# Issuing each step of a node update one edge group ahead of its waiter, with two tiles in flight

## The reference, cut to what matters

```python
for l in range(2):                                   # N=3125 nodes, E=100000 edges, D=128, H=8, FF=512
    q, k, v = (linear maps of layernorm(x) and of the node degree)
    att = einsum(q[dst], k[src]) / scale             # per edge and head, clipped to +-50
    ex = exp(att - m[dst]);  alpha = ex / segment_sum(ex, dst)[dst]
    aggr = segment_sum(v[src] * alpha, dst)          # edges and one self loop per node
    x = x + (aggr @ Wo + bo)
    h = gelu(layernorm(x) @ W1 + b1)
    x = x + (h @ W2 + b2)
out = layernorm(x0 + x)
```

## The kernel before

| group | DVE | PE | ACT |
|---|---|---|---|
| even | prod ... att, add_ffn(k-1), one-hots, evacuate, msg, normalise_x3(k-1), share_out(k) | gather_q, sum_further, sum_pair, transpose_z2(k-1), transpose_ag(k), project_next(k-1), project_out(k) | weights, scale_x3(k-1), copy_z2T(k-1), copy_agT(k), one_hots |
| odd | next_row(k-1), add_attention(k), prod ... att, normalise_x2(k), one-hots, evacuate, msg | gather_q, sum_further, transpose_z1(k), hidden(k), sum_pair, project_ffn(k) | scale_x2(k), weights, copy_z1T(k), gelu(k), one_hots |

## Time and profile before

### The profile page before, as it was taken

The page is one execution under the profiler, slowest core; times in us unless marked ns, Lnnn a source line. Parts: engine busy times, 40 slices in busy tenths (PEclk is TensorE's granted clock), DMA queues, the critical chain, the costliest instruction groups (busy, mean ns, idle before and its releaser), DMA issues.

```text
span 2410.0 us, 44174 instructions
## 1 busy us (share of the span) xinstructions
PE 1539.5 (64%) x11737; PEld 1367.1 (57%) x11738; DVE 1474.6 (61%) x2506; ACT 921.0 (38%) x1652; POOL 1506.8 (63%) x1584
## 2 busy tenths in 40 slices
PE   6656555666677676667664556555666666666766
PEld 4545554555666665566653455555555566655665
DVE  8685556566565565656647656565665666555665
ACT  3232222223444454445533222322334444444543
POOL 2557777777776565556407777777777666565550
PEclk8776778677788788889876767777788888787787
DMA  3444555555444444434305555555544444343430
GB/s 76 129 144 158 158 157 158 156 157 159 151 148 134 124 137 125 121 118 135 95 9 173 158 155 157 162 158 157 157 152 152 136 133 129 115 131 117 123 118 5
DMA packets 120426, 321.52 MB, mean 133 GB/s; under 512 B 31458, under 2 KB 43862, under 8 KB 120348
## 3 DMA queue, kind: packets, MB, share of 16 engines
q0 software_dynamic: 75072, 205.10, 28.7%
q1 hardware_dynamic: 44438, 113.89, 14.7%
q10 hardware_dynamic: 838, 1.60, 0.3%
HBM read 311.92 MB, written 8.55 MB: 133 GB/s over the span
## 4 chain that ended last, share of the span: by engine, by line
POOL 29%; PE 26%; issue 16%; DVE 14%; ACT 7%; DVEq 5%; ACTq 2%; DMA 1%; POOLq 0%; SPq 0%
POOL kv L529 29%; PE ps L1280 12%; PE ps L1266 7%; DVE msg L1067 3%; DVE prod L1041 3%; ACT dist L657 2%; DVEq L345 2%; ACT hotT L660 2%; DVE dots L1044 2%; PE ps L1237 2%; DVE q_parts L800 1%; PE ps L1254 1%; PE ps L1243 1%; ACT L629 1%; DVE spot L974 1%
## 5 line engine op out<-in xcount | busy, mean ns | idle before, releaser
L529 POOL DMA_INDIRECT kv<-kv_tab,src_idx x1564 | 1482.4, 948 | 792.8 <-issue 457.0
L1280 PE MATMUL ps<-msg,hot 128*128 128x136 f32 x3904 | 670.8, 339 | 333.6 <-DVE msg L1067 292.5
L1266 PE MATMUL ps<-q_parts,hotT 128*128 x5856 | 562.9, 271 | 451.8 <-DVE prod L1041 256.8
L1280 PEld LDWEIGHTS ps<-msg,hot 128*128 128x128 f32 x3904 | 619.8, 241 | 376.6 <-DVE msg L1067 188.4
L1266 PEld LDWEIGHTS ps<-q_parts,hotT 128*128 x5856 | 499.4, 124 | 512.6 <-issue 492.1
L1041 DVE TENSOR_TENSOR prod<-kv,ps 128x1024 f32<-128x1024 f32 x196 | 239.2, 1220 | 294.3 <-DMA kv<-kv_tab,src_idx 263.7
L949 DVE SCALAR_TENSOR_TENSOR hot<-dst_col,neg_base,ps 128x1024 f32<-128x1024 f32 x244 | 312.0, 1279 | 127.5 <-issue 124.6
L657 ACT ACTIVATE dist<-dst_rows,neg_node 128x1024 bf16<-128x1024 int32 x244 | 280.1, 1148 | 152.3 <-issue 137.7
L664 ACT ACTIVATE msg<-att 128x64 f32<-128x64 f32 x196 | 49.1, 250 | 619.5 <-DVE att L1051 617.4
L660 ACT ACTIVATE hotT<-dist 128x1024 bf16 x244 | 257.8, 1057 | 44.6 <-ACT dist L657 43.7
L1067 DVE TENSOR_TENSOR msg<-kv,ps 128x1024 f32<-128x1024 f32 x196 | 238.1, 1215 | 22.8 <-issue 19.3
(11 more groups left out here) (205 smaller groups left out, 1154.3 us busy)
## 6 DMA issues: line engine op xcount, KB each, us to landing
dst_rows<-in_dst SPq DMA_DIRECT2D x194, 512.0 KB, 4.1
kv<-kv_tab,src_idx POOLq DMA_INDIRECT x1564
kv_tab<-qkv SPq DMA_DIRECT2D x27, 128.0 KB
kv_tab<-qkv SPq DMA_DIRECT2D x3, 768.0 KB, 3.7
out<-z SPq DMA_DIRECT2D x25, 64.0 KB
dst_rows<-in_dst SPq DMA_DIRECT2D x2, 336.0 KB, 3.6
hot<-in_L_gnn_W SPq DMA_DIRECT2D x2, 256.0 KB
w<-in_L_gnn_W SPq DMA_DIRECT2D x2, 256.0 KB
```

Of the source, the lines that this page charges most:

```text
L529: pool.indirect_dma_start(kv[:, u, c, :], None, kv_tab[l][:, :], bass.IndirectOffsetOnAxis(ap=src_idx[:, c, at(g)], axis=0)).then_inc(kv_i ...
L1266: last = MM(qd[:, c * P:(c + 1) * P], hotT[:, bass.ds(pr % 2, 1), c * P:(c + 1) * P], q_parts[:, at(t), k * D:(k + 1) * D], start=first an ...
L1280: last = MM(agg, hot[:, u % 2, c, :], msg[:, u % 2, c, :], start=(c == 0), stop=(c == GC - 1))
```

## The change

The steps of a slot keep their work and move to other places in the groups: each is issued about a group before the step on another engine that waits for it, so that a slot now spans five groups and two tiles are under way at once. With k the slot of the even group and its odd follower:

| group | DVE | PE | ACT |
|---|---|---|---|
| even | prod ... att, share_out(k), one-hots, msg, evacuate, next_row(k-2) | gather_q, sum_further, hidden(k-1), transpose_ag(k), project_next(k-2), sum_pair, project_ffn(k-1), project_out(k) | copy_z1T(k-1), copy_z2T(k-2), weights, copy_agT(k), gelu(k-1), one_hots |
| odd | prod ... att, add_ffn(k-1), add_attention(k), one-hots, msg, evacuate, normalise_x3(k-1), normalise_x2(k) | gather_q, sum_further, sum_pair, transpose_z2(k-1), transpose_z1(k) | weights, scale_x3(k-1), scale_x2(k), one_hots |

`evacuate` also moves from before `msg` to behind it, in all groups. DVE's loop over the slot groups has twelve groups instead of four. Buffers x3, z1T and z2T are added, PSUM banks are dealt anew, SP stores a slot's row one group later, and the slot table takes tiles that are finished one group earlier than before. The core of the diff:

```diff
-        in_slot = {"agT": bank(5, P), "o": bank(5, P), "z1T": bank(4, P), "h": [ps[:, 5, c * P:(c + 1) * P] for c in range(FC)],
-                   "y": bank(6, P), "z2T": bank(4, P), "qkv": bank(6, 3 * D)}
+        in_slot = {"agT": bank(5, P), "o": bank(5, P), "z1T": bank(5, P), "h": [ps[:, 6, c * P:(c + 1) * P] for c in range(FC)],
+                   "y": bank(6, P), "z2T": bank(4, P), "qkv": bank(4, 3 * D)}
...
-                link(nc.vector.tensor_copy(least, low[:, a:b:2]))
-                link(nc.vector.tensor_tensor(least, least, low[:, a + 1:b:2], ALU.min))
+                link(nc.vector.tensor_copy(least, low[:, a - 1:b - 1:2]))
+                link(nc.vector.tensor_tensor(least, least, low[:, a:b:2], ALU.min))
...
+                # ACT
+                def edge_group(word, d, g, u, r, n, slot=None):
+                    even, odd = (slot is not None and u % 2 == k for k in (0, 1))
+                    if even and not_before(slot, 1):
+                        copy_z1T(slot - 1, 0, in_slot)
+                    if even and not_before(slot, 2):
+                        copy_z2T(slot - 2, 0, in_slot)
+                    weights(u, g)
+                    if odd and not_before(slot, 1):
+                        scale_x3(slot - 1, 0)
+                    if odd and opens(slot):
+                        scale_x2(slot, 0)
+                    if even and opens(slot):
+                        copy_agT(slot, 0, in_slot)
+                    if even and not_before(slot, 1):
+                        gelu(slot - 1, 0, in_slot)
+                        log_and_exp()
+                    if not isinstance(g, int) or g + 2 < NG:
+                        one_hots(word, d + 2, r, n)
...
                     # DVE
                     nc.vector.tensor_tensor(att[:, :], clipped[:, :], not_nan[:, :], ALU.mult).then_inc(att_done[l], 1)
-                    if odd and not closing:
-                        normalise_x2(slot, 0)
-                    if even and not opening:
+                    if even and opens(slot):
+                        share_out(slot_tile(dve, slot), slot, 0)
+                        wait_for_number(dve, ag_done[l], slot + 1)
+                    if odd and not_before(slot, 1):
+                        passed = slot_tile(dve, slot - 1)
                         add_ffn(passed, slot - 1, 0, in_slot)
+                    if odd and opens(slot):
+                        add_attention(slot_tile(dve, slot), slot, 0, in_slot)
...
                     one_hot(u, g, tile_of(dve, a, shift))
-                    if not opened:
-                        evacuate(a, last_shift)
                     if ahead:
                         word(d + 1)
                     dve.wait_ge(exp_done[l], g + 1)
                     nc.vector.tensor_tensor(half[:, :, 0:D]...).then_inc(msg_done[l], 1)
-                    if even:
-                        if not opening:
-                            normalise_x3(passed, slot - 1, 0)
-                        if not closing:
-                            dve.wait_ge(evac_done[l], a + 2)
-                            share_out(current, slot, 0)
+                    if not opened:
+                        evacuate(a, last_shift)
+                    if odd and not_before(slot, 1):
+                        normalise_x3(passed, slot - 1, 0)
+                    if odd and opens(slot):
+                        normalise_x2(slot, 0)
+                    if even and not_before(slot, 2):
+                        next_row(slot_tile(dve, slot - 2), slot - 2, 0, in_slot)
...
+                with dve.Fori(2 * FIRST_SLOT // TURN_OF_DVE + 1, 2 * SLOT_END // TURN_OF_DVE) as i:
+                    word = pair_words(dve, TURN_OF_DVE * i)
+                    for u in range(TURN_OF_DVE):
+                        edge_group(u % SLOTS, ..., ahead=u < TURN_OF_DVE - 1, slot=number + u // 2)
...
                     # PE, after gather_q and sum_further
+                    if even and not_before(slot, 1):
+                        hidden(slot - 1, 0, in_slot)
+                    if even and opens(slot):
+                        transpose_ag(slot, 0, in_slot)
+                    if even and not_before(slot, 2):
+                        project_next(slot - 2, 0, in_slot)
                     pe.wait_ge(msg_done[l], g + 1)
                     sum_pair(u, word(d - 1)[0])
+                    if even and not_before(slot, 1):
+                        project_ffn(slot - 1, 0, in_slot)
+                    if even and opens(slot):
+                        project_out(slot, 0, in_slot)
+                    if odd and not_before(slot, 1):
+                        transpose_z2(slot - 1, 0, in_slot)
+                    if odd and opens(slot):
+                        transpose_z1(slot, 0, in_slot)
```

More of the change, by code:

```diff
@@ L163, in gnn_program @@
         rsum = sb("rsum", [P, TAIL, H])
-        one_of_each = {name: sb(name, [P, D]) for name in ("ag", "agT", "x2", "z2", "zT")}
+        one_of_each = {name: sb(name, [P, D]) for name in ("ag", "agT", "x2", "x3", "z1T", "z2", "z2T")}
         spot = sb("spot", [P, TAIL, 2, 10])
@@ L358, in after, with not_before, opens @@
                 eng.wait_ge(semaphore, n)
+        def not_before(slot, n):
+            return not isinstance(slot, int) or slot >= n
+        def opens(slot):
+            return not isinstance(slot, int) or slot < NSLOT
         def slot_tile(eng, j):
@@ L461, in _ @@
                         store(slot_tile(sp, n), 0)
-                for n in range(NSLOT - 2, NSLOT):
+                for n in range(NSLOT - 3, NSLOT):
                     ready(n + 1)
@@ L614, in copy_z1T @@
                     act.wait_ge(z1T_ps[l], n + 1)
-                    nc.scalar.activation(zT[s], banks["z1T"], ACT.Copy).then_inc(z1T_done[l], 1)
+                    nc.scalar.activation(z1T[s], banks["z1T"], ACT.Copy).then_inc(z1T_done[l], 1)
                 def gelu(n, s, banks):
@@ L836, in slot_words_out @@
                 link(nc.vector.tensor_scalar(last, last, float(NT - TAIL), None, ALU.min))
-                for g in (NG - 2, NG - 1):
+                for g in range(2 * SLOT_END - 1, NG):
                     link(nc.vector.tensor_tensor(last, last, low[:, g:g + 1], ALU.min))
@@ L1019, in next_row, with edge_group @@
                                                        in1=banks["qkv"].unsqueeze(1), op0=ALU.mult, op1=ALU.add).then_inc(next_done, 1)
-                def edge_group(u, i, g, word, d, ahead=True, slot=None, opening=False, closing=False):
+                def edge_group(u, i, g, word, d, ahead=True, slot=None):
                     half = msg[:, u % 2, :, :]
                     b, shift = word(d)
-                    odd = slot is not None and u % 2 == 1
-                    even = slot is not None and u % 2 == 0
-                    if even:
-                        if not opening:
-                            passed = slot_tile(dve, slot - 1)
-                        if not closing:
-                            current = slot_tile(dve, slot)
-                    if odd:
-                        if not closing:
-                            current = slot_tile(dve, slot)
-                        if not opening:
-                            next_row(slot_tile(dve, slot - 1), slot - 1, 0, in_slot)
-                        if not closing:
-                            add_attention(current, slot, 0, in_slot)
+                    even, odd = (slot is not None and u % 2 == k for k in (0, 1))
                     last_group = isinstance(g, int) and g == NG - 1
@@ L1236, in hidden @@
                     for c in range(FC):
-                        last = MM(banks["h"][c], w1g[:, l, c * P:(c + 1) * P], zT[s], start=True, stop=True)
+                        last = MM(banks["h"][c], w1g[:, l, c * P:(c + 1) * P], z1T[s], start=True, stop=True)
                     last.then_inc(h_ps[l], 1)
@@ L1286, in sum_further, with pe_group @@
                             sum_pair(u, pr)
-                def pe_group(u, g, word, d, more=True, slot=None, opening=False, closing=False):
-                    odd = slot is not None and u % 2 == 1 and not closing
-                    even = slot is not None and u % 2 == 0
+                def pe_group(u, g, word, d, more=True, slot=None):
+                    even, odd = (slot is not None and u % 2 == k for k in (0, 1))
                     if more:
@@ L1329, in _ @@
                 word = pair_words(pe, 0)
-                pe_group(0, NG - 2, word, NG - 2, slot=NSLOT, closing=True)
-                pe_group(1, NG - 1, word, NG - 1, more=False)
+                for g in range(NG - 2, NG):
+                    pe_group(g % SLOTS, g, word, g, more=g < NG - 1, slot=NSLOT)
+                project_next(NSLOT - 1, 0, in_slot)
                 sum_further(1, word(NG - 2)[0], word(NG - 1)[0])
```

94 lines of the change are left out of this document (29 added, 65 removed).

## The result

The changed kernel takes 2220.97 us (median of four runs, 2219.82 to 2223.71) where the kernel before takes 2409.41 us (four runs; the 2408.93 us above is of three of them); the ratio is 0.922, with a 95% interval from 0.9204 to 0.9236. The forecast was 2222 us. The profiled execution has a span of 2217.9 us at a mean clock of 0.804 (0.778 before).

The account below looks back on a forecast made before the run. PE, ACT, PE round trips and late sums that make DVE wait bound the slot stages, above POOL's 480 us a layer. (612 - 518) + (602 - 512) + 3 = 187 saved from 2412.0 gives 2225, 2222 at the median; range 2160 to 2300.

Parts of the forecast that it names:

- The slot of three kinds: Two-group slots priced by extra pair: none 20.0 us, in the even group 21.0, in the odd 22.1; 505.7 us together.
- other idle time, kept as it was: DVE's idle time in a slot besides the priced waits, such as sequencer work: 3.0, 3.6 or 3.4 us by kind.
- added reads: Slot tile numbers now read by DVE in mid-group, behind a wait: 1.0 us more a slot.
- waits for PE: DVE's remaining waits: 0.6 or 1.7 us in slots with an extra pair, plus 12 us a layer for PE's clock.
- rival 4: The next_row wait only moves to add_attention; only the evacuation gains, 53 us a layer: 2303 us, chance 0.04.
- three steps are missing: Layer 1's slot stage lacks three steps and has one more add: 512 us against layer 0's 518.
- The loop of twelve: DVE's loop over twelve groups: fewer table re-reads at turn heads book 7 us gained; cold straight code costs 5 a layer.
- rival 5: Larger loop body stalls 1.23 us at each branch, 89 us in all: 2311 us, chance 0.04.
- The closing groups: After the slot groups, group 96's 5 us wait goes and next_row comes behind group 97: -3 us a layer.
- POOL's floor everywhere: Both slot stages fall to POOL's 480 us: time 2155 us, chance 0.12.
- PE the bound: PE stays at its lower clock half the time, a slot costs 24 us: about 2347 us, chance 0.11.
- a closed ring: ACT's z copies block its exponentials, making msg late in each slot: 2462 us at 5 us a slot, chance 0.05.

Follow-up runs that it names:

- e1: The changed kernel with add_attention(k) put back to the head of the odd group, ahead of prod: 2380.38 us, ratio 0.9868 to the kernel before.
- e2: The changed kernel with the evacuation put back ahead of msg: 2260.1 us, ratio 0.9365 to the kernel before.
- e3: The kernel before with only the evacuation moved behind msg: 2350.27 us, ratio 0.9745.
- e4: The changed kernel with DVE's loop over four groups instead of twelve: 2224.26 us, ratio 0.9219 to the kernel before.
- e5: The changed kernel with DVE's table reads moved behind the issue of prod and of the reduction, on a slow chip: 3372.68 us, ratio 0.9898.
- e12: The changed kernel with early table reads and next_row(k-2) moved to the odd group, a repeat on a slow chip: 3329.3 us, ratio 1.0003.
- e9: The changed kernel with early table reads and next_row(k-2) moved to the odd group, run again on another slow chip: 3331.77 us, ratio 1.0015.

## Why the prediction was right

**Where the time is, and the floor.** The slot stages alone gave, as the prediction read from the windows; the plain stage did not move.

**The slot of three kinds.** By the starts of prod, the 24 slots of layer 0 take on average 19.3 us without an extra pair (six, priced at 20.0), 21.2 with one in the even group (eleven, 21.0) and 23.1 with one in the odd group (seven, 22.1). Together that is 511 us; the prediction had 505.7 + 12 = 518. The first kind goes below POOL's 20.0 (18.1 in the window of groups 78 and 79), since POOL had run ahead while slots with extra pairs were slow; the price of 20.0 as a floor for each slot was too strict.

**The terms.** Added up over the 24 slots, the prediction's terms and what the profile of the changed kernel shows for them are (us, layer 0):

| term | booked | measured |
|---|---|---|
| DVE busy | 370.8 | 367.7 |
| other idle time, kept as it was | 81.4 | 50.9 |
| added reads | 24.0 | 47.8 |
| waits for PE | 30.5 | 44.6 |
| POOL's floor in the slots without an extra pair | 10.2 | 0 |
| sum | 517 | 511.0 |

The mechanism was right; four of the five sizes were off by 10 to 31 us, two up and two down. With the two that were too small put right alone, the stage would have been forecast at some 555 us, with the two that were too large at 476. That the sum is within 7 us is in part luck.

**The evacuation and next_row.** 52.9 to 15.5 us and 92.2 to 19.3 us. "The next_row wait gone" was too much: it stands in 13 of the slots, 0.9 to 2.5 us long, where PE is behind. e1 and e2 put single steps back, for 155 and 35 us. The evacuation alone, which rival 4 priced at 53 us a layer, gives 62 us in both (e3).

**The added reads** were booked at 1.0 us a slot and measure about 2: 14.9 + 14.6 + 7.2 us of issue before rsum, x2 and x3, and 11.1 us before the one-hot behind wait_for_number, 47.8 us for 24 slots. The idle time that was "kept" made up for it: the issue before the one-hot fell from 28.1 to 20.0 (heads of turns, booked elsewhere), that before prod from 13.2 to 4.0 us, DVE's 8.7 us wait for ACT's scale is not among the waits any more, and 6.9 us of issue before msg are gone; against them 10.2 us of waits for gathers stand where 3.8 did.

**PE.** Booked at 12 us a layer over the waits of the slot kinds (0.6 x 11 + 1.7 x 7 = 18.5), 30.5 in all; DVE's waits for PE add up to 19.3 + 15.5 + 5.4 + 3.3 + 1.1 = 44.6 us in layer 0. The clock rose from 0.82 to 0.87 in that stage and PE's busy time fell from 425.7 to 391.9 us, so PE is busy 77% of the stage, not over 80% as expected. With e1's wait put back it is 0.80 in that stage again, and 0.84 with most of next_row's left (e3); e2 and e4 have 0.88 and 0.89. So the long waits had cost PE its clock, and that they went made PE cheaper. (The sum of 3.34 us from which the factor 1.6 was taken ran at a mean of 0.61, so it is a little under the price of the lower level.)

**Layer 1** was expected 6 us under layer 0 and is 6 us over it. The step that failed there is "three steps are missing": it counted their work as gained. With next_row gone, DVE is at the prod of the odd group 0.8 us after the end of msg instead of 2.1 (means of 23 slots), and so comes to add_ffn earlier; PE's FFN projection stands behind the sum, which waits for msg, and ends 5.3 us after msg instead of 5.0, though PE has less to do. So DVE waits there for PE, 33.1 us against 5.4 in layer 0. A step that is left out on the engine that waits gives little when the result it waits for comes no sooner.

**The loop of twelve** was booked at -7 for its heads and +10 for cold code. Neither is what was measured. The heads are 14 us a layer on DVE, of which e4 shows nothing in the median; the cold code is some 4 to 5 us in the run. The price of 1.23 us was read from a row that shows something else: what stands at 997.38 in the earlier trace rows is no stall at a branch but ACT's second table load of the slot (L629), and the instruction behind it starts as it ends:

```profile
997.32 1.28 ACT L629 ACT_TABLE_LOAD   x1
998.61 1.15 ACT L657 ACTIVATE dist<-dst_rows,neg_node 128x1024 bf16<-128x1024 int32 x1
```

So none of the rows of the kernel before shows a stall of this kind, though the prediction says that the trace agrees with one; the term of 5 us a layer and rival 5's 89 us were built on it. The Trainium skill, "Runtime: NRT & Kernel Launch", section "Instruction fetch mechanics", has straight code fetched ahead and a taken branch outside the held blocks stall. The trace of the changed kernel agrees, with 77 packets against 41 and 1.0 to 1.36 us at the back edges. Rival 5 would have needed 1.23 us at each of the branches in between. There, the heads of turns aside, no gap of issue in layer 0 is over 1.04 us.

**The closing groups** were booked at -3 us a layer: layer 0 gave 5.4 us behind its slot groups, layer 1 nothing (48.8 us to the end instead of 48.0).

**Rivals.** 1 (POOL's floor everywhere, 2155): the stages stay 31 and 37 us above it, and behind group 53 DVE waits for no gather, so POOL is not what holds them. Whether DVE's reads or PE's order gives next was to be told by e5 to e12 and is not settled; e4 says that both do. 2 (PE the bound): not at twice the price for half the time; DVE's waits for PE are 44.6 of 511 us, and the clock rose. 3 (a closed ring): ACT's exponentials are not late; msg waits for ACT once, 0.2 us. 4: refuted by DVE's 1.1 us of waiting for the attention output, and by e2, which gains 153 us without the evacuation's move. 5: see above.

## What to carry to other kernels

Where an engine that works in order asks another for a result, look at what stands in its queue between the request and the first instruction that needs the answer; moving the consumer behind half a group of independent work took some 3 us out of each of 48 slots here (e1: 155/48), and moving one step back gave 155 of 188 us away. Work that is added on the engine that waits may cost nothing (e4), and work that is left out there may gain nothing (layer 1), as long as another engine's result is late. Price the steps by kind (with and without the irregular work), take busy time and idle time apart for each, and ask of every piece of idle time whether it is a wait that goes or sequencer work that moves along. A register read costs its full 0.5 to 1 us behind a wait (14.9 us before the 24 rsum); read behind the issue of prod and of the reduction, in e5, no gap is left before rsum. And look up what an idle stretch is on its engine's own timeline before it is priced: the "issue" of the earlier trace rows was a table load.

## What had not been expected of the hardware

On four of the five chips used for experiments the kernel before took about 3310 to 3410 us instead of 2410, within a percent on each. The rows of e9 show a part of the cause: PE starts one matmul in 2.1 to 2.8 us for some 10 us at a time, with 1.0 to 2.4 us of idle time that is put down to nobody, and the mean granted clock is 0.68 instead of 0.80. In e5's slot stage 93 GB/s moved instead of 153, which may be no more than the consequence: POOL took the same 0.95 us a gather and spent a third of the span waiting for messages. The clock alone does not give it either: at a mean granted clock of 0.61 a sum of 16 took 3.34 us, and at 0.50 here 14. Why these chips do so stays open.
